# AFNO layers on one core: the MLP's products of a period put side by side, a second buffer for the spectrum's activation, and another order of the slots

## Chip, core and metric

One Trainium2 chip, and one of its cores. The metric is the device time of one execution of the whole program in microseconds (us), the median of several runs; lower is better.

## What is computed

The input is a batch of 4 images of 64 channels, 128 x 128, in fp32. One box-filter layer comes first, then four AFNO blocks, then two more box-filter layers. The change touches the AFNO blocks alone. One block, cut to what matters:

```python
xn = _ln(xp, ln1w, ln1b)                          # xp: channels last
xf = jnp.fft.rfft2(xn, axes=(1, 2), norm='ortho')
o1 = relu(complex product of xf with w1, + b1)    # 64 x 64 per frequency
o2 = complex product of o1 with w2, + b2
o2 = o2 * ((|o2r| > 0.01) | (|o2i| > 0.01))
x = residual + irfft2(o2)
xp2 = _ln(x, ln2w, ln2b)
h = jax.nn.gelu(xp2 @ mw1 + mb1, approximate=False)   # 64 -> 256
x = x + h @ mw2 + mb2                                 # 256 -> 64
```

Lines 3 to 5 are shortened to words: the reference writes the real and imaginary parts out.

## The kernel before

`afno_layers` holds all four blocks of all four images in one loop. A **run** n is one block of one image; there are 16 (`RUNS`). A run has 16 **periods** q (`BLOCKS`), and each period has four **slots** s. In period q of run n every engine carries one block of 8 image rows through one stage of the MLP of run n, and in its slots does parts of the Fourier work, mostly that of run n + 1 (`parts`, `parts_in`). So the MLP of one image and the spectrum of the next lie beside each other. Q = 16n + q numbers the MLP's blocks.

The MLP's pieces are, on TensorE (PE): `turn` (four 128-column transposes into `turned`, L1734), `mlp_up(Q, 0)` and `mlp_up(Q, 1)` (the two halves of the hidden layer, each two 512-column products on 64 rows of the array, into the one buffer `wide`, L1714), `mlp_down` (four 512-column products with 64 output rows, into `result`, L1725) and `turn_back` (transposes into `result`, L1740). ScalarE (ACT) does `gelu` out of `wide` (L1539), `operand` (the copy of `turned`, L1545), `mlp_delta` (the bias on `result`, L1552) and `square` (the squares for the layer norm's sums, L1573). VectorE (DVE) adds the result to the image in `residual` (L1428), sums the rows in `sum_up` (two reductions, L1445 and L1447) and takes the inverse root in `root` (12 small steps, L985 to L1005). GpSimd (POOL) does `normalise` (L1270), `next_y` (L1282) and `fold` (L1293, L1295).

`mlp_up(Q, 1)` writes `wide` and so waits for gelu(Q, 0), and `mlp_up(Q + 1, 0)` for gelu(Q, 1). `mlp_down(i)` waits for residual(i - 1), since both use `result`.

The Fourier work of a run goes over the slots of the period so:

- q 0, 1 (slot 3) and q 4 (slots 1 and 2): `inverse` 4 to 7 of run n. PE forms an even and an odd part of 8 rows (L1642, L1646). ACT copies the odd part to `odd` (L1495), DVE adds in three steps (L1366, L1367, L1371), and POOL subtracts `odd` from the upper rows (L1258), which frees `odd` for the next copy.
- q 4 (slot 3) to q 5 (slot 2): `forward`, 16 groups of four transforms (L1660), copied out to `g` by DVE and ACT in turn (L1126 to L1129 and L1502).
- q 5 (slot 3) to q 10 (slot 1): `spectrum`, steps t = 0 to 18. A step has on PE the second transform fh(t) (`dft_h`, L1689, into bank 0), the first mixing product mix1(t-1) (L1680, into bank 2) and the second mix2(t-2) (L1671, into bank 3). ACT does relu o1(t-1) (L1519) and then the copy xf(t) out of bank 0 (L1526). DVE adds a bias in o2(t-2) (L1397), and makes the mask of step t-3 (L1414, L1417); POOL applies it (L1308, L1312). mix1(t) waits for xf(t). fh(0) waits for all copies of `forward` and for a DVE memset (L1390) behind them.
- q 11: `backward`, 16 groups (L1704), copied out by DVE (L1422) and ACT (L1531).
- q 12 (slots 0, 1, 3) and q 13 (slot 1): `inverse` 0 to 3.

What sets the order is written out by hand: each engine has a loop over the periods that calls the MLP's pieces and `parts(n, q, s, ...)` in a fixed order, and every engine works its list in that order. PE's list, in a period of the spectrum, is mlp_up(Q, 0), slot 0, turn_back(Q-2), turn(Q+1), slot 1, mlp_up(Q, 1), slot 2, mlp_down(Q-1), slot 3. ACT's is gelu(Q, 0), slot 0, operand(Q+1), a square, slot 1, gelu(Q, 1), slot 2, mlp_delta(Q-1), slot 3. In runs whose layer is the last (`fresh`), ACT has copies of the next image besides (`fill_stage`, L1584).

## Time and profile before

| | |
|---|---|
| median of 3 runs | 3581.37 us (3580.07 to 3583.23) |
| the profiled execution's own time | 3576.51 us |
| its span | 3574.7 us |
| PE busy in the span | 3260.3 us (91%) |
| DVE, ACT, POOL busy | 2413.1, 2210.3, 1648.1 us (68%, 62%, 46%) |
| mean granted TensorE clock | 0.966 |

The profiled execution is 4.9 us below the median and 1.8 us above its own span. Busy times are sums over the whole program; matmuls are pipelined, so a busy PE may still be waiting inside a matmul's record. The AFNO part with its MLP lies from about 410 to 3160 us of the span.

### The profile page before, as it was taken

What the parts mean: (1) busy time and instruction counts of PE and PEld (TensorE: products, weight loads), DVE (VectorE), ACT (ScalarE), POOL (GpSimd) and SP (SyncE); (2) the same over time, 40 slices, a digit from 0 to 9 for tenths busy, and PEclk for the clock granted to TensorE, in tenths of its full rate; (3) what the DMA queues carried; (4) which work ended last, traced back from release to release, by engine and by line L of the source; (5) the groups of instructions that cost most, each with busy time, mean ns of one, the idle gap of its engine ahead of it and who ended that gap; (6) DMA issues with size and microseconds to landing.
All of it is one profiled execution on the core that took longest, in us unless ns stands there. A gap on an engine that the chain in (4) does not pass through costs nothing. (4 is left out here: it accounts for less than half of the span.)

```text
span 3574.7 us, 52777 instructions
## 1 busy us (share of the span) xinstructions
PE 3260.3 (91%) x18285; PEld 1965.9 (55%) x18285; DVE 2413.1 (68%) x4148; ACT 2210.3 (62%) x3477; POOL 1648.1 (46%) x1389
## 2 busy tenths in 40 slices
PE   6946699999999999998999999999999999979689
PEld 2735364647464646464646464646464646334257
DVE  4956676767676676666666767676767665636677
ACT  3954466666666666667666666666656565646468
POOL 4445545464645454545454545555454543210242
PEclk7968899999999999999999999999999999989889
DMA  9850001010101010313120101111111111356898
GB/s 326 273 183 24 30 31 65 31 65 31 65 30 65 30 65 30 118 48 142 48 89 31 65 30 65 36 65 41 55 42 54 42 54 42 138 193 188 265 301 239
DMA packets 250280, 334.08 MB, mean 93 GB/s; under 512 B 22305, under 2 KB 195617, under 8 KB 242609
## 3 DMA queue, kind: packets, MB, share of 16 engines
q1 hardware_dynamic: 241664, 315.29, 26.0%
...
## 5 line engine op out<-in xcount | busy, mean ns | idle before, releaser
L1539 ACT ACTIVATE images<-a_wide,a_up_b 128x1024 f32<-128x1024 f32 x512 | 569.4, 1112 | 187.9 <-PE a_wide L1714 186.5
L1714 PE MATMUL a_wide<-images 64*128 64x512 f32 x2048 | 579.7, 641 | 37.1 <-ACT images L1539 36.4
L1312 POOL TENSOR_TENSOR images<-a_o,a_mag 128x256 f32<-128x256 f32 (+1 forms) x512 | 360.8, 731 | 401.7 <-DVE a_mag L1417 401.7
L1725 PE MATMUL a_result<-images 128*64 128x512 f32 x2048 | 495.9, 604 | 31.9 <-DVE images L1428 31.7
L1270 POOL TENSOR_TENSOR images<-images,a_stat 128x512 f32<-128x512 f32 x256 | 268.2, 1049 | 520.4 <-DVEq L1462 503.3
L1397 DVE TENSOR_TENSOR a_o<-a_bank,a_mix_b 128x512 f32<-128x512 f32 (+1 forms) x272 | 181.1, 666 | 266.8 <-PE a_bank L1671 260.8
L1689 PEld LDWEIGHTS a_bank<-a_dft_h,a_g 128*128 128x128 f32 x2080 | 272.4, 191 | 129.0 <-issue 129.0
L1671 PEld LDWEIGHTS a_bank<-a_mix,a_o 128*128 128x128 f32 x2080 | 252.8, 191 | 149.7 <-issue 130.9
L1519 ACT ACTIVATE a_o<-a_bank,a_mix_b 128x512 f32<-128x512 f32 (+2 forms) x272 | 181.7, 668 | 202.9 <-PE a_bank L1680 202.9
L1671 PE MATMUL a_bank<-a_mix,a_o 128*128 128x128 f32 x2080 | 298.0, 285 | 5.4 <-DVE a_o L1397 3.2
L1725 PEld LDWEIGHTS a_result<-images 128*64 128x64 f32 x2048 | 128.0, 136 | 313.5 <-issue 290.5
L1447 DVE TENSOR_REDUCE a_stat<-a_sq 128x16 f32<-128x1024 f32 x240 | 290.3, 1210 | 9.4 <-ACT a_sq L1573 8.3
L1258 POOL TENSOR_TENSOR images<-images,a_odd 128x512 f32<-128x512 f32 (+1 forms) x128 | 161.6, 1262 | 288.4 <-DVE images L1367 279.4
L1660 PE MATMUL a_bank<-dft_w,images 128*128 128x128 f32 x2048 | 246.6, 279 | 48.1 <-POOL images L1295 46.1
L1552 ACT ACTIVATE images<-a_result,a_down_b 128x512 f32<-128x512 f32 x256 | 175.8, 687 | 185.4 <-PE a_result L1725 185.1
L1714 PEld LDWEIGHTS a_wide<-images 64*128 64x128 f32 x2048 | 157.3, 185 | 238.9 <-issue 202.6
L1445 DVE TENSOR_REDUCE a_stat<-images 128x16 f32<-128x1024 f32 x232 | 281.3, 1212 | 4.8
L1660 PEld LDWEIGHTS a_bank<-dft_w,images 128*128 128x128 f32 x2048 | 236.0, 193 | 83.7 <-POOL images L1295 46.1
L1428 DVE TENSOR_TENSOR images<-a_result,images 128x512 f32<-128x512 f32 x256 | 175.3, 685 | 156.0 <-PE a_result L1740 155.9
L1689 PE MATMUL a_bank<-a_dft_h,a_g 128*128 128x128 f32 x2080 | 277.3, 275 | 1.8 <-DVE a_g L1390 1.8
L1680 PE MATMUL a_bank<-a_xf,a_mix_fold 128*128 128x512 f32 (+1 forms) x544 | 270.0, 578 | 0.8 <-ACT a_xf L1526 0.8
L1573 ACT ACTIVATE a_sq<-images 128x1024 f32<-128x1024 f32 x216 | 227.5, 1053 | 66.5 <-DVE a_stat L1447 42.8
...
## 6 DMA issues: line engine op xcount, KB each, us to landing
...
```

The costliest lines, as they stand in the source:

```text
L1270: G.tensor_tensor(rows(y2[:, i % 2]), x[:, row:row + HB], r[:, :, None].broadcast_to([P, HB, C]), ALU.mult).then_inc(s_y2, 1)
L1312: ins = G.tensor_tensor(y[n % 2][:, :, to].rearrange("p c k -> p k c"), o2[:, j % 3, lo:4, r], mask[:, lo:4], ALU.mult)
L1445: V.tensor_reduce(stat[:, 0, r % SETS, kind - 1, u * SH:(u + 1) * SH], strip, AX.X, ALU.add)
L1447: V.tensor_reduce(stat[:, 1, r % SETS, kind - 1, u * SH:(u + 1) * SH], squares_of(r, kind, u), AX.X, ALU.add).then_inc(s_sq_read, 1)
L1539: A(hidden[:, i % 2, j], wide[:], ACT.Gelu, bias=up_b2[:, l, j:j + 1]).then_inc(s_hid, 1)
L1573: A(squares_of(r, kind, u), strip, ACT.Square).then_inc(s_sq, 1)
L1660: mm = M(bank[i % 4][:, c * P:(c + 1) * P], y[n % 2][:, 4 * i + c, :], dft_w[:], start=True, stop=True)
L1671: mm = M(bank[3][:, k * P:(k + 1) * P], o1[:, k * P:(k + 1) * P], mix2[:, l], start=True, stop=True)
L1680: M(bank[2][:, 0:cols], mix1_fold[:, l], xf[:, 0:cols], start=True, stop=True).then_inc(s_mix1, 1)
L1689: mm = M(bank[0][:, k * P:(k + 1) * P], g[:, first_kw(t) + k].rearrange("p r c -> p (r c)"), dft_h[:], start=True, stop=True)
L1714: mm = M(wide[:, half * BANK:(half + 1) * BANK], up_fold[cs, l, j * P:(j + 1) * P], yc[cs, i % 2], start=True, stop=True)
L1725: mm = M(result[half * C:(half + 1) * C, :], down[:, l, j, :], hidden[:, i % 2, j, half * BANK:(half + 1) * BANK], start=j == 0, stop=j == ...
```

## The change

1. **Order on PE.** mlp_up(Q, 1), mlp_down(Q-1) and mlp_up(Q+1, 0) are called one behind the other, after slot `window_after(q)` (3, but 2 in q 4 and 12, and 1 in q 5, where mlp_up(Q+1, 0) stays behind slot 3). ACT's gelu(Q, 1) and mlp_delta(Q-1) go to the same place.
2. **Order inside a spectrum step.** mix2(t-2) is called behind mix1(t-1) and fh(t), no longer ahead of them. `o1` has two homes (`o1_of`): the odd steps write it to `odd`. Relu o1(j) waits for mix2(j-2) instead of mix2(j-1).
3. **First slot.** Slot 0 is called ahead of the transposes (on DVE ahead of `residual`, on ACT ahead of `operand`) in q 5 to 10 and 12 (`SLOT_FIRST`), and behind them elsewhere. Of the slots 0 that hold work this moves that of q 11 on DVE and ACT alone.
4. **DVE's sums.** The two reductions of `sum_up` are called in two slots that follow each other, and the root of q 1 behind slot 2.

No instruction is added or taken out, apart from waits. In the diff below the pieces stand in this order: the tables, `o1_of`, DVE's loop, ACT's `inverse`, `spectrum` and loop, and PE's loop. PE's `spectrum` is left out: its block of mix2 (`j = t - 2`) moves as it is from the top to behind fh and reads `o1_of(j)`.

```diff
+SLOT_FIRST = (5, 6, 7, 8, 9, 10, 12)
+def window_after(q):
+    return {4: 2, 5: 1, 12: 2}.get(q, 3)
...
+        def o1_of(j):
+            return odd[:].rearrange("p h c -> p (h c)") if j % 2 else o1[:]
...
+                    late = 3 if q == 5 else 2 if q % 4 == 3 and fresh(n) else 1
...
+                        if s - late in (0, 1):
+                            for strip in strips[-1:]:
+                                sum_up(*strip, s - late)
...
-                            if q == 1 and s == 1:
+                            if q == 1 and s == 2:
                                 root(r, range(ROOT_STEPS))
...
                     act.wait_ge(s_x_up, INVERSES * n + j)
+                    if j == 0:
+                        act.wait_ge(s_mix2, N_CHUNK * (n + 1) - 1)
...
-                        if j >= 1:
-                            act.wait_ge(s_mix2, before + j)
+                        if before + j >= 2:
+                            act.wait_ge(s_mix2, before + j - 1)
+                        if j == 1 and n:
+                            act.wait_ge(s_x_up, INVERSES * n)
...
-                    parts(n, q, 1, inverse, forward, spectrum, backward)
-                    if mlp:
-                        gelu(Q, 1)
...
+                        if s == 1 and q == 12:
+                            for strip in strips_at(n, q)[:1]:
+                                square(*strip)
...
+                        if s == window_after(q):
+                            if 0 <= Q < BLOCKS * RUNS:
+                                gelu(Q, 1)
+                            if 0 <= Q - 1 < BLOCKS * RUNS:
+                                mlp_delta(Q - 1)
...
-                    parts(n, q, 1, inverse, forward, spectrum, backward)
-                    if mlp:
-                        mlp_up(Q, 1)
-                    parts(n, q, 2, inverse, forward, spectrum, backward)
-                    if 0 <= Q - 1 < BLOCKS * RUNS:
-                        mlp_down(Q - 1)
-                    parts(n, q, 3, inverse, forward, spectrum, backward)
+                    for s in range(4):
+                        if s or q not in SLOT_FIRST:
+                            parts(n, q, s, inverse, forward, spectrum, backward)
+                        if s == window_after(q):
+                            if 0 <= Q < BLOCKS * RUNS:
+                                mlp_up(Q, 1)
+                            if 0 <= Q - 1 < BLOCKS * RUNS:
+                                mlp_down(Q - 1)
+                        if s == max(window_after(q), 3 if q == 5 else 0) and 0 <= Q + 1 < BLOCKS * RUNS:
+                            mlp_up(Q + 1, 0)
```

What it does to the lists, at three places. The line numbers of the changed kernel differ: L1742 and L1753 are mlp_up and mlp_down, L1688 `forward`, L1708 fh, L1699 mix1, L1717 mix2, L1768 and L1762 turn_back and turn.

PE, from the last quarter of `forward` in q 5 to slot 1 of q 6; before:

```order
L1714 MATMUL a_wide<-images 128x512 x2
L1660 MATMUL a_bank<-dft_w,images 128x128 x16
L1725 MATMUL a_result<-images 64x512 x4
L1689 MATMUL a_bank<-a_dft_h,a_g 128x128
L1714 MATMUL a_wide<-images 128x512 x2
L1680 MATMUL a_bank<-a_xf,a_mix_fold 128x128
```

and now:

```order
L1742 MATMUL a_wide<-images 128x512 x2
L1753 MATMUL a_result<-images 64x512 x4
L1688 MATMUL a_bank<-dft_w,images 128x128 x16
L1708 MATMUL a_bank<-a_dft_h,a_g 128x128
L1742 MATMUL a_wide<-images 128x512 x2
L1699 MATMUL a_bank<-a_xf,a_mix_fold 128x128
```

mlp_down stood between the last group of `forward` and fh(0); now fh(0) is the next product behind that group.

PE, slots 1 to 3 of q 6 with the products of the MLP (the first row is turn); before:

```order
L1734 MATMUL a_turned<-ident,images 128x128 x4
L1671 MATMUL a_bank<-a_mix,a_o 128x128
L1680 MATMUL a_bank<-a_xf,a_mix_fold 128x512
L1689 MATMUL a_bank<-a_dft_h,a_g 128x128 x4
L1714 MATMUL a_wide<-images 128x512 x2
L1671 MATMUL a_bank<-a_mix,a_o 128x128 x4
L1680 MATMUL a_bank<-a_xf,a_mix_fold 128x512
L1689 MATMUL a_bank<-a_dft_h,a_g 128x128 x4
L1725 MATMUL a_result<-images 64x512 x4
```

and now:

```order
L1762 MATMUL a_turned<-ident,images 128x128 x4
L1699 MATMUL a_bank<-a_xf,a_mix_fold 128x512
L1708 MATMUL a_bank<-a_dft_h,a_g 128x128 x4
L1717 MATMUL a_bank<-a_mix,a_o 128x128
L1699 MATMUL a_bank<-a_xf,a_mix_fold 128x512
L1708 MATMUL a_bank<-a_dft_h,a_g 128x128 x4
L1717 MATMUL a_bank<-a_mix,a_odd 128x128 x4
L1699 MATMUL a_bank<-a_xf,a_mix_fold 128x512
L1708 MATMUL a_bank<-a_dft_h,a_g 128x128 x4
L1717 MATMUL a_bank<-a_mix,a_o 128x128 x4
L1742 MATMUL a_wide<-images 128x512 x2
L1753 MATMUL a_result<-images 64x512 x4
```

Three steps of the spectrum follow each other with no product of the MLP between; between fh(t) and mix1(t) stands mix2(t-2) alone.

ACT, from the first `inverse` of q 12 to slot 3; before:

```order
L1495 ACTIVATE a_odd<-a_bank 128x512 [waits a_x_up,a_iw]
L1545 ACTIVATE images<-a_turned 128x512 [waits a_up,a_tr]
L1495 ACTIVATE a_odd<-a_bank 128x512 [waits a_x_up,a_iw]
L1539 ACTIVATE images<-a_wide,a_up_b 128x1024 [waits a_up]
L1573 ACTIVATE a_sq<-images 128x1024 [waits a_sq_read,a_x]
L1552 ACTIVATE images<-a_result,a_down_b 128x512 [waits a_back,a_down]
```

and now:

```order
L1520 ACTIVATE a_odd<-a_bank 128x512 [waits a_mix2,a_x_up,a_iw]
L1572 ACTIVATE images<-a_turned 128x512 [waits a_up,a_tr]
L1520 ACTIVATE a_odd<-a_bank 128x512 [waits a_x_up,a_iw]
L1600 ACTIVATE a_sq<-images 128x1024 [waits a_sq_read,a_x]
L1566 ACTIVATE images<-a_wide,a_up_b 128x1024 [waits a_up]
L1579 ACTIVATE images<-a_result,a_down_b 128x512 [waits a_back,a_down]
```

The square, which waits for DVE's sums into x, now stands ahead of gelu(Q, 1). In q 4 both copies of the odd part stand ahead of gelu(Q, 1) in the same way; before, it stood between them.

## Rows read from the trace of the kernel before

**Rows 1.** Busy time by engine over one run; PE, PEld, DVE, ACT, POOL.

```profile
1121.00:1297.33 176.33, 170.98 (x972) 103.07 (x973) 123.39 (x216) 110.38 (x164) 91.06 (x77) 1.00 0.14 49
```

**Rows 2.** Timeline, PE, spectrum, q 7: start us, us, engine, line.

```profile
1194.35 1.05 PE L1689 MATMUL a_bank<-a_dft_h,a_g 128*128 128x128 f32 x8
1195.24 0.60 PE L1740 MATMUL a_result<-ident,images 128*128 128x128 f32 x4
...
1196.11 1.06 PE L1671 MATMUL a_bank<-a_mix,a_o 128*128 128x128 f32 x8
1197.00 1.02 PE L1680 MATMUL a_bank<-a_xf,a_mix_fold 128*128 128x512 f32 x2
1197.87 1.05 PE L1689 MATMUL a_bank<-a_dft_h,a_g 128*128 128x128 f32 x8
1198.85 1.13 PE L1714 MATMUL a_wide<-images 64*128 64x512 f32 x4
1199.91 1.16 PE L1671 MATMUL a_bank<-a_mix,a_o 128*128 128x128 f32 x8
```

**Rows 3.** Timeline, PE's turn and what ACT does behind it, q 6.

```profile
1180.32 0.60 PE L1734 MATMUL a_turned<-ident,images 128*128 128x128 f32 x4
...
1180.96 0.60 ACT L1545 ACTIVATE images<-a_turned 128x512 f32<-128x512 f32 x1 [0.27 <-PE a_turned L1734]
1181.45 1.05 ACT L1573 ACTIVATE a_sq<-images 128x1024 f32<-128x1024 f32 x1
...
1183.11 0.61 ACT L1526 ACTIVATE a_xf<-a_bank 128x512 f32<-128x512 f32 x1
```

**Rows 4.** Timeline, the first image's spectrum, which has no MLP beside it.

```profile
344.64 0.69 ACT L1519 ACTIVATE a_o<-a_bank,a_mix_b 128x512 f32<-128x512 f32 x1 [1.31 <-PE a_bank L1680]
345.38 1.16 PE L1671 MATMUL a_bank<-a_mix,a_o 128*128 128x128 f32 x8
```

**Rows 5.** Timeline, all engines, end of q 5.

```profile
1175.31 1.94 PE L1725 MATMUL a_result<-images 128*64 128x512 f32 x8
1175.42 1.33 ACT L1502 ACTIVATE a_g<-a_bank 64x252 f32<-64x252 f32 x4 [0.45 <-PE a_bank L1660]
...
1176.90 0.17 DVE L1390 MEMSET a_g<- 1x128 f32 x1 [0.82 <-ACT a_g L1502]
...
1177.22 0.46 PE L1689 MATMUL a_bank<-a_dft_h,a_g 128*128 128x128 f32 x2
```

**Rows 6.** Timeline, q 4.

```profile
1150.30 0.66 PE L1734 MATMUL a_turned<-ident,images 128*128 128x128 f32 x4 [1.09 <-POOL images L1270]
...
1157.19 0.60 ACT L1495 ACTIVATE a_odd<-a_bank 128x512 f32<-128x512 f32 x1 [2.29 <-POOL images L1258]
```

**Rows 7.** Timeline, q 12.

```profile
1274.30 1.94 PE L1725 MATMUL a_result<-images 128*64 128x512 f32 x8
1274.42 1.11 ACT L1539 ACTIVATE images<-a_wide,a_up_b 128x1024 f32<-128x1024 f32 x1
1274.67 0.69 DVE L1371 TENSOR_TENSOR images<-a_bank,images 128x512 f32<-128x512 f32 x1
...
1275.43 1.05 ACT L1573 ACTIVATE a_sq<-images 128x1024 f32<-128x1024 f32 x1
...
1276.17 1.13 PE L1642 MATMUL a_bank<-a_g,a_idft_e 128*128 128x512 f32 x2
```

**Rows 8.** Timeline: mlp_up and DVE's root in q 1, mlp_down in q 2.

```profile
1130.70 1.13 PE L1714 MATMUL a_wide<-images 64*128 64x512 f32 x4 [0.28 <-ACT images L1539]
...
1133.49 1.10 DVE L985 SCALAR_TENSOR_TENSOR a_stat<-a_stat 128x64 f32<-128x64 f32 x1
...
1140.26 1.94 PE L1725 MATMUL a_result<-images 128*64 128x512 f32 x8 [1.15 <-DVE images L1428]
```

**Rows 9.** Timeline, DVE, a mask of the spectrum beside POOL's work, and one without.

```profile
1195.02 0.29 DVE L1417 TENSOR_SCALAR a_mag<-a_mag 128x256 f32<-128x256 f32 x1
...
1198.53 1.94 DVE L1417 TENSOR_SCALAR a_mag<-a_mag 128x256 f32<-128x256 f32 x1
```

More of the change, by code:

```diff
@@ L1588, in _ @@
                     Q = BLOCKS * n + q
-                    mlp = 0 <= Q < BLOCKS * RUNS
-                    if mlp:
+                    if 0 <= Q < BLOCKS * RUNS:
                         gelu(Q, 0)
-                    parts(n, q, 0, inverse, forward, spectrum, backward)
+                    if q in SLOT_FIRST:
+                        parts(n, q, 0, inverse, forward, spectrum, backward)
                     if 0 <= Q + 1 < BLOCKS * RUNS:
                         operand(Q + 1)
-                    if q != 12 and not (q % 4 == 3 and fresh(n)):
-                        for strip in strips_at(n, q):
-                            square(*strip)
@@ L1664, in spectrum @@
                     before, l = N_CHUNK * n, layer_of(n)
-                    j = t - 2
-                    if 0 <= j < N_CHUNK:
-                        pe.wait_ge(s_o1, before + j + 1)
-                        if j >= 1:
-                            pe.wait_ge(s_o2, before + j)
-                        for k in range(chunk(j)):
-                            mm = M(bank[3][:, k * P:(k + 1) * P], o1[:, k * P:(k + 1) * P], mix2[:, l],
-                                   start=True, stop=True)
-                        mm.then_inc(s_mix2, 1)
                     j = t - 1
@@ L1691, in spectrum @@
                         mm.then_inc(s_fh, 1)
+                    j = t - 2
+                    if 0 <= j < N_CHUNK:
+                        pe.wait_ge(s_o1, before + j + 1)
+                        if j >= 1:
+                            pe.wait_ge(s_o2, before + j)
+                        for k in range(chunk(j)):
+                            mm = M(bank[3][:, k * P:(k + 1) * P], o1_of(j)[:, k * P:(k + 1) * P], mix2[:, l],
+                                   start=True, stop=True)
+                        mm.then_inc(s_mix2, 1)
                     if t == 8:
@@ L1753, in _ @@
                         turn(Q + 1)
[L1754 to L1762 removed]
+                    for s in range(4):
+                        if s or q not in SLOT_FIRST:
+                            parts(n, q, s, inverse, forward, spectrum, backward)
+                        if s == window_after(q):
+                            if 0 <= Q < BLOCKS * RUNS:
+                                mlp_up(Q, 1)
[3 more added lines that the diff above has]
+                            mlp_up(Q + 1, 0)
         clear(nc, sems)
```

73 lines of the change are left out of this document (36 added, 37 removed).

## The prediction

> **What bounds the kernel now.** I read the table of busy times first, then one run of the loop (16 periods), then its timeline instruction by instruction. In a run of 176.3 us PE is busy 171.0, and the clock is granted in full (1.00); the other engines are at 52 to 70% [rows 1]. So PE bounds the run, and what counts is (a) how densely its products follow each other and (b) where it waits. Run follows run in the timeline in nearly the same way, so every figure below is for one run and is multiplied by 15, the runs that have both an MLP and the next spectrum beside it (run 15 has no next one).
>
> PE's prices, start to start [rows 2]: mix1 0.87, fh 0.89, mix2 0.89, turn_back and turn 0.87 together, mlp_up 1.06. mlp_down takes 1.87, from its start to that of the next product [rows 7]. Before, the steps of the spectrum in q 6 to 9 are never next to each other: a product of the MLP or the transposes stands between each pair, and no product there shows an idle time [rows 2]. That cover is what the change takes away.
>
> **What is saved: changes of shape.** fh before mlp_up lasts 0.98 to the next start, but 0.89 before turn_back; mix2 lasts 1.16 behind mlp_up, but 1.06 behind turn [rows 2]. So going into the MLP's half-array products costs 0.09 and coming out 0.10, together 0.19 a stretch. By the loop there are 33 stretches a run before (16 of mlp_up(Q, 1), 7 of mlp_down apart from it, in q 4 to 9 and 11, and 10 of mlp_up(Q+1, 0) apart from mlp_down, in q 0, 1, 4 to 9, 11, 12) and 17 after (q 5 keeps two). 16 x 0.19 = **3.0 us saved**. The Trainium skill's TensorEngine Tiling (Array Packing), Key Properties, says that changing the tiling mode drains the array; mlp_up is tiled by rows and mlp_down by columns, so by that rule a merged stretch still drains between them, half of the saving goes, and the sum below rises by 1.5 a run. The rows here do not show such a drain: mlp_up takes 1.06 before mix2 [rows 2], and that is also what it takes before mlp_down elsewhere in the timeline.
>
> **What is saved in q 0 to 2.** `inverse` 4 and 5 now come ahead of mlp_up(Q, 1) and mlp_down, 1.06 + 1.87 = 2.9 us nearer to the transposes. That hides the wait for gelu(Q, 0) (0.28 in q 1 [rows 8]), and lets DVE do its additions earlier. At the end of this stretch mlp_down of q 2 waits 1.15 for DVE [rows 8], so the gain is DVE's: turn_back of q 1 comes 0.5 earlier, and from there the chain residual, two sums, root, `inverse` 5, residual is shorter by 0.3 because `inverse` 4 is no longer in it and by 0.85 if the root's first step (1.10 beside POOL's normalise [rows 8]) runs alone, in about a quarter of that as the steps behind it do. 1.6 in all, of which 0.4 was counted as shape: **1.2 saved**. Bounds 0.3 to 1.2.
>
> **What is lost, five waits.**
>
> *fh(0), q 5.* It needs the last copies of `forward` and the memset behind them. ACT's four copies of the last group begin 0.11 after mlp_down's start, the memset is at 1176.90, and fh(0) starts at 1177.22, 1.91 after mlp_down started, which itself took 1.87 of that [rows 5]. So mlp_down just covers the copies. Now nothing stands between the last group and fh(0): PE idles **1.9**. This one I take as certain.
>
> *mlp_up(Q+1, 0), q 4.* It needs gelu(Q, 1), and ACT now does both odd copies first. The second waits for POOL and starts 1157.19 - 1150.30 = 6.89 after turn [rows 6]; copy 0.60 [rows 6], gelu 1.11 [rows 7] and about 0.1 to PE put mlp_up at 8.6 to 8.7. PE would reach it at 0.44 + four 512-column products of 0.87 + 0.1 + 1.06 + 1.87 = 6.95. **1.7 lost**; behind it is `forward`, which moves with it. Bounds 1.0 (if POOL comes earlier) to 1.9.
>
> *mix1(2), q 6.* Behind turn ACT has operand, square, relu, xf. From turn's start operand comes at 0.64, the square at 1.13 and xf, with a relu before it and no gap, at 2.79; it ends at 3.40 [rows 3]. A result of ACT reaches PE's weight load 0.05 later (345.33 to 345.38 [rows 4]): 3.45. PE, with mix1(1), fh(2) and the one-column mix2(0) (a quarter of 0.89) is ready at 0.44 + 0.87 + 0.89 + 0.22 = 2.4. About 1.1 lost, and 0.15 for two smaller gaps as below: **1.2**. Before, mlp_up and a mix2 lay in there. Bounds 0.8 to 1.3.
>
> *q 7 to 9.* The same with a full mix2: PE wants the weights of mix1 at 0.44 + 0.87 + 0.89 + 0.89 less 0.11 for the load, 2.98 after turn; xf, behind operand, square and relu, is there at 3.3: 0.34. For steps that follow each other without a square: fh's record 1.05, latency 0.04, xf 0.60, latency 0.05 make 1.74 from fh's start, and the weights are wanted at 0.89 + 0.89 - 0.11 = 1.67: 0.07. So 0.41 a period, three times 1.2; all three shape savings of 0.38 are used up by it. For DVE in q 7: a mask that lasts 1.94 beside POOL's work, not 0.29 [rows 9], now lies in a slot of 2.7 us together with a bias add, a reduction and half of `sum_up` (1.2), which makes the next add, and mix2 two steps on, late by about 0.3. **1.5** together, bounds 0.6 to 4 (rival 3).
>
> *mlp_up(Q+1, 0), q 12.* gelu(Q, 1) now stands behind the square, and the square waits for DVE's third addition: it starts at 1275.43, whatever PE does [rows 7]. Square 1.0, gelu 1.11, 0.1 to PE: 1277.6. PE reaches the product at 1274.30 + 1.87 = 1276.17 [rows 7]. 1.45 lost. Then `inverse` 2 and 3 come later, ACT has a square and a gelu between their odd copies, so the second copy comes about 0.5 later still, DVE's sums wait for it and mlp_down of q 14 waits for DVE. With the shape saving of 0.2 given back there: **2.1**. Bounds 1.2 to 2.1: the waits of q 14 and 15 could take up some of it.
>
> The two homes of o1 cost nothing: `odd` is free long before. Splitting `sum_up` costs nothing; its halves lie under PE. Slot 0 of q 11 on DVE and ACT: their copies have 1.8 us for two groups of `backward`. In q 11 and 10 nothing is lost beyond 0.1.
>
> **Sum.** -3.0 - 1.2 + 1.9 + 1.7 + 1.2 + 1.5 + 2.1 = +4.2 us a run, 15 x 4.2 = 63. The profiled execution would go from 3576.5 to 3639.5, and the median, which lay 4.9 above it, from 3581.4 to **3644**. Left out are two runs where ACT has image copies of 2 us in the way (a few us more) and the first image's spectrum, whose steps get shorter by some 0.1 (under 2 us less). With all bounds at the low end the sum is +2.2 (-3.0 - 0.3 + 1.9 + 1.0 + 0.8 + 0.6 + 1.2), or with the q 0 to 2 gain in full +1.3; at the high end about +7.5.
>
> **Rivals.**
> 1. *The cover was never needed (faster).* If ACT's copies reach PE in time in q 4, 6 to 9 and 12, because PE drifts against ACT and each wait paid once moves the later ones into place, only fh(0) stays: -3.0 - 1.2 + 1.9 = -2.3, times 15 is -35: 3547. It is decided at mix1 behind a square: xf would have to end within 3.0 us of turn and not 3.4. For it: PE has 2.9 us more in one piece, in which ACT can catch up. Against it: operand, square, relu and xf come behind turn by order, back to back [rows 3]. 0.15.
> 2. *Only the waits outside the steps (about as before, or a little slower).* If the steps run at 2.64 with no gap and the rest holds, +4.2 - 2.7 = +1.5, or 3604: 0.16. If also q 4 costs nothing, -0.2, or 3578: 0.09.
> 3. *DVE becomes the bound.* The masks held by POOL cost 1.65 each more [rows 9]; in a slot with a sum DVE then has 4.5 us (add, reduction and mask 1.7, the hold 1.65, half a sum 1.2) against PE's 2.7, and mix2 two steps on is late by 0.9 instead of 0.3. Once in each of q 6 to 9 that is 2.7 a run more, 40 in all: 3684. For it: POOL works through q 6 and 7. Against it: the sum is now split, and the 4 us of the MLP let DVE catch up. 0.10.
>
> That the change does not do what it says I give no chance: the lists show it.
>
> **How the numbers follow.** My forecast has 0.50. Slower by over 0.2% (7 us, about what runs of this kernel can tell) is 0.50 + 0.16 + 0.10 = 0.76; within 0.2% is 0.09; faster is 0.15. The likeliest case alone gives 3612 (+2.1 a run) to 3670. The range takes in 3578, 3604 and 3684 and leaves out the faster case: 3575 to 3690.
>
> **What would show it.** In the new profile the run should last about 180.5 us, not 176.3. fh(0) should show 1.9 us idle behind a DVE memset; mlp_up in q 4 and 12 waits of 1.7 and 1.4 for ACT's gelu; mix1 small waits for xf, the largest, 1.1, in q 6; q 11 should be 0.4 shorter, and mlp_down of q 2 come 1.6 earlier. If mix1 shows no waits, rival 1 or 2 is right; if mix2 waits for DVE's add in q 6 to 9, rival 3.

## Result and the profile after

| | before | changed |
|---|---|---|
| median of 4 runs | 3581.19 us (3580.07 to 3583.23) | 3700.67 us (3693.03 to 3707.34) |
| ratio | | 1.0332, interval 1.0311 to 1.0353 |
| span of the profiled execution | 3574.7 us | 3705.6 us |
| PE, DVE, ACT, POOL busy | 3260.3, 2413.1, 2210.3, 1648.1 us | 3280.5, 2422.3, 2199.0, 1649.2 us |

It is 3.3% slower, in the direction forecast, but the loss is 119 us where 63 were forecast, and 3700.7 lies outside the range (3575 to 3690). PE's busy time rose by 20 us although its list does the same products with fewer changes of shape, and the runs of the changed kernel spread over 14 us, not 3. The first comes from the clock, as the experiments show; the second stays open. The profiled execution of the changed kernel (3707.3 us) is the slowest of its four, 6.7 us above the median, and what follows is read from it.

The waits of the changed kernel by PE in the loop of the layers (columns: engine, output and line that waited, what for; total us, times, longest us):

```profile
PE a_wide L1742 <- ACT images L1566: 79.0, 108, 3.1
PE a_result L1753 <- DVE images L1438: 40.4, 44, 2.0
PE a_bank L1699 <- ACT a_xf L1553: 39.9, 45, 1.2
PE a_turned L1762 <- POOL images L1280: 32.0, 27, 13.5
PE a_bank L1708 <- DVE a_g L1400: 29.3, 16, 1.8
PE a_bank L1732 <- POOL images L1322: 8.8, 16, 4.6
```

mlp_up's wait for gelu (L1742), mix1's for xf (L1699) and fh's for the memset (L1708) are new or larger, as forecast (36.4, 0.8 and 1.8 us before, in the same view). To see where a run loses its time I take the starts of `turn` from PE's timeline, one a period, and compare the distance from each to the next in both kernels (medians of eight runs without image copies; forecast from the terms of the prediction, each change of shape put in its period). A run takes 184.5 us, not 176.3.

| turn to turn | before | changed | difference | forecast |
|---|---|---|---|---|
| q 0 to 4 | 27.7 | 26.5 | -1.25 | -1.6 |
| q 4 to 5 | 16.09 | 17.39 | +1.31 | +1.3 |
| q 5 to 6 | 13.94 | 17.41 | **+3.47** | +1.7 |
| q 6 to 7 | 15.35 | 16.16 | +0.81 | +0.8 |
| q 7 to 8 | 16.47 | 17.35 | **+0.88** | +0.3 |
| q 8 to 9 | 16.02 | 16.01 | 0.0 | 0.0 |
| q 9 to 10 | 15.13 | 16.01 | **+0.88** | 0.0 |
| q 10 to 12 | 27.7 | 27.9 | **+0.18** | -0.4 |
| q 12 to 0 | 27.9 | 29.8 | +1.94 | +1.9 |
| run | 176.3 | 184.5 | +8.2 | +4.2 |

Four rows are as forecast, to 0.1 us; q 5, 7 and 9 hold 3.2 of the 4 us missed, and q 10 and 11 another 0.6. PE's timeline of the changed kernel in q 5, which answers to [rows 5], and the same stretch in windows (columns: window, its length, busy us and instructions of each engine, granted clock, DMA):

```profile
1209.78 3.62 PE L1688 MATMUL a_bank<-dft_w,images 128*128 128x128 f32 x31
1215.23 0.46 PE L1708 MATMUL a_bank<-a_dft_h,a_g 128*128 128x128 f32 x2 [1.83 <-DVE a_g L1400]
1215.62 1.78 PE L1742 MATMUL a_wide<-images 64*128 64x512 f32 x4
1217.34 0.79 PE L1699 MATMUL a_bank<-a_xf,a_mix_fold 128*128 128x128 f32 x2
1217.92 1.75 PE L1708 MATMUL a_bank<-a_dft_h,a_g 128*128 128x128 f32 x8
1219.51 0.60 PE L1768 MATMUL a_result<-ident,images 128*128 128x128 f32 x4
```

```profile
1213.00:1215.20 2.20, 0.40 (x4) 0.21 (x2) 1.31 (x5) 1.30 (x4) 0.00 (x0) 1.00 0.00 0
1215.20:1217.00 1.80, 1.77 (x6) 0.60 (x6) 1.80 (x2) 0.28 (x1) 0.00 (x0) 0.71 0.03 9
1217.00:1219.00 2.00, 2.00 (x10) 1.67 (x9) 1.72 (x7) 1.37 (x2) 0.00 (x0) 0.50 0.00 0
1219.00:1219.60 0.60, 0.60 (x5) 0.60 (x5) 0.00 (x0) 0.00 (x0) 0.00 (x0) 0.69 0.00 0
1219.60:1223.00 3.40, 3.00 (x21) 2.28 (x19) 1.05 (x3) 3.01 (x6) 0.00 (x0) 1.00 0.00 0
```

The idle before fh(0) is 1.83 us, as forecast. But right behind it the granted clock goes from 1.00 (2.4 GHz) to 0.50 (1.2 GHz), and mlp_up takes 1.78 us, not 1.13, and fh(1) 1.75, not 1.05. Before, the clock was 1.00 from 432 to 3180 us. In the changed kernel it falls in q 5 in 13 of 15 runs, and five times more in runs 6 to 8, in or behind PE's waits of 2.0 to 3.1 us around the image copies.

ACT in q 7, which answers to [rows 3], DVE's residual there, and what PE's mix1 does:

```profile
1236.74 0.60 ACT L1572 ACTIVATE images<-a_turned 128x512 f32<-128x512 f32 x1 [1.17 <-PE a_turned L1762]
1238.13 1.06 ACT L1600 ACTIVATE a_sq<-images 128x1024 f32<-128x1024 f32 x1 [0.79 <-DVE images L1438]
```

```profile
1235.87 0.69 DVE L1407 TENSOR_TENSOR a_o<-a_bank,a_mix_b 128x512 f32<-128x512 f32 x1 [2.82 <-PE a_bank L1717]
...
1237.20 0.29 DVE L1427 TENSOR_SCALAR a_mag<-a_mag 128x256 f32<-128x256 f32 x1
1237.41 0.68 DVE L1438 TENSOR_TENSOR images<-a_result,images 128x512 f32<-128x512 f32 x1
```

```profile
1240.30 1.12 PE L1699 MATMUL a_bank<-a_xf,a_mix_fold 128*128 128x512 f32 x2 [0.95 <-ACT a_xf L1553]
```

In q 7 and 9 the square reads the image that `residual` writes. DVE does slot 0's add, reduction and mask first, and the add waits for mix2, which now comes last in slot 0. So the square waits 0.79, xf comes as much later, and mix1 waits 0.95, not the 0.34 forecast for any square. In q 8, where the square does not wait for `residual`, the period is as long as before.

q 4 and 12, where the forecast held (ACT's second odd copy and PE's mlp_up in q 4; PE in q 12):

```profile
1192.04 0.60 ACT L1520 ACTIVATE a_odd<-a_bank 128x512 f32<-128x512 f32 x1 [3.89 <-POOL images L1268]
```

```profile
1193.79 1.13 PE L1742 MATMUL a_wide<-images 64*128 64x512 f32 x4 [1.63 <-ACT images L1566]
...
1319.96 1.13 PE L1742 MATMUL a_wide<-images 64*128 64x512 f32 x4 [1.36 <-ACT images L1566]
```

Two smaller waits, the first product of `backward` in q 11 and mlp_down in q 14:

```profile
1292.51 14.56 PE L1732 MATMUL a_bank<-a_dft_hi,images 128*128 128x128 f32 x128 [0.28 <-POOL images L1322]
...
1333.55 1.94 PE L1753 MATMUL a_result<-images 128*64 128x512 f32 x8 [1.33 <-DVE images L1438]
```

The first, for POOL's mask, is not there in an ordinary run before; the second was 0.88. So of the 1.94 lost in q 12 to 15 some 0.45 lies in q 14, where the prediction had it too.

### The profile page after: what moved, and what is told of

Same layout as the page of the kernel before. It is cut to its first block and busy times, and to the rows that moved or that the text cites. A ratio compares the mean times of both kernels' runs of the same rounds, so it can differ in the third digit from the quotient of the medians.

```text
span 3705.6 us, 52776 instructions
## 1 busy us (share of the span) xinstructions
PE 3280.5 (89%) x18285; PEld 1989.3 (54%) x18285; DVE 2422.3 (65%) x4148; ACT 2199.0 (59%) x3477; POOL 1649.2 (45%) x1389
## 5 line engine op out<-in xcount | busy, mean ns | idle before, releaser
L1742 PE MATMUL a_wide<-images 64*128 64x512 f32 x2048 | 586.3, 648 | 81.5 <-ACT images L1566 79.0
L1753 PE MATMUL a_result<-images 128*64 128x512 f32 x2048 | 498.5, 607 | 40.4 <-DVE images L1438 40.4
L1708 PEld LDWEIGHTS a_bank<-a_dft_h,a_g 128*128 128x128 f32 x2080 | 284.0, 199 | 147.3 <-issue 147.3
L1742 PEld LDWEIGHTS a_wide<-images 64*128 64x128 f32 x2048 | 158.8, 186 | 369.0 <-issue 352.7
L1753 PEld LDWEIGHTS a_result<-images 128*64 128x64 f32 x2048 | 128.4, 136 | 380.0 <-issue 380.0
L1699 PE MATMUL a_bank<-a_xf,a_mix_fold 128*128 128x512 f32 (+1 forms) x544 | 292.6, 621 | 40.8 <-ACT a_xf L1553 39.9
L1708 PE MATMUL a_bank<-a_dft_h,a_g 128*128 128x128 f32 x2080 | 288.4, 283 | 29.3 <-DVE a_g L1400 29.3
L1688 PE MATMUL a_bank<-dft_w,images 128*128 128x128 f32 x2048 | 241.6, 278 | 47.3 <-POOL images L1305 46.2
L1688 PEld LDWEIGHTS a_bank<-dft_w,images 128*128 128x128 f32 x2048 | 233.9, 193 | 71.5 <-POOL images L1305 46.3
L1732 PE MATMUL a_bank<-a_dft_hi,images 128*128 128x128 f32 x2048 | 235.3, 277 | 8.8 <-POOL images L1322 8.8
L1732 PEld LDWEIGHTS a_bank<-a_dft_hi,images 128*128 128x128 f32 x2048 | 232.2, 194 | 12.7 <-POOL images L1322 12.7
L1376 DVE TENSOR_TENSOR images<-a_bank,images 128x512 f32<-128x512 f32 x128 | 88.1, 688 | 202.1 <-PE a_bank L1674 147.4
```

Source lines behind the costliest of these rows:

```text
L1688: mm = M(bank[i % 4][:, c * P:(c + 1) * P], y[n % 2][:, 4 * i + c, :], dft_w[:], start=True, stop=True)
L1699: M(bank[2][:, 0:cols], mix1_fold[:, l], xf[:, 0:cols], start=True, stop=True).then_inc(s_mix1, 1)
L1708: mm = M(bank[0][:, k * P:(k + 1) * P], g[:, first_kw(t) + k].rearrange("p r c -> p (r c)"), dft_h[:], start=True, stop=True)
L1732: mm = M(bank[i % 4][:, c * P:(c + 1) * P], y[n % 2][:, 4 * i + c, :], dft_hi[:], start=True, stop=True)
L1742: mm = M(wide[:, half * BANK:(half + 1) * BANK], up_fold[cs, l, j * P:(j + 1) * P], yc[cs, i % 2], start=True, stop=True)
L1753: mm = M(result[half * C:(half + 1) * C, :], down[:, l, j, :], hidden[:, i % 2, j, half * BANK:(half + 1) * BANK], start=j == 0, stop=j == ...
```

## Experiments

Three questions: does the idle in q 5 bring the lower clock; does each wait belong to one edit; and what is left of the change if each is repaired. Where an expectation says step 5, it means period q 5. The table gives for each kernel the difference to the kernel before, us per run, by the same turns, and in how many of the 15 periods q 5 of its profiled execution the clock fell. Each batch of runs had the kernel before beside it, at 3577.7 (a), 3580.2 (b), 3579.7 (c), 3579.4 (d) and 3579.2 us (e), and at 3581.2 beside the changed kernel; so a difference of medians between batches is sure to some 4 us only.

| kernel | median | q 0-4 | q 4 | q 5 | q 6 | q 7 | q 8 | q 9 | q 10-11 | q 12-15 | low clock in q 5 |
|---|---|---|---|---|---|---|---|---|---|---|---|
| changed | 3700.7 | -1.3 | +1.3 | +3.5 | +0.8 | +0.9 | 0 | +0.9 | +0.2 | +1.9 | 13 of 15 |
| a1 MLP ahead of fh(0) | 3650.5 | -1.3 | +1.3 | -0.2 | +0.8 | +0.9 | 0 | +0.9 | +0.2 | +1.9 | 0 |
| a2 idle alone | 3614.6 | 0 | 0 | +1.9 | 0 | 0 | 0 | 0 | 0 | 0 | 5 |
| a3 gelu first, q 12 | 3666.1 | -1.2 | +1.3 | +1.9 | +0.8 | +0.9 | 0 | +0.9 | +0.2 | +0.5 | 5 |
| a4 stretch between, q 4 | 3709.4 | -1.3 | +1.5 | +3.5 | +0.8 | +0.9 | 0 | +0.9 | +0.2 | +1.9 | 12 |
| b1 residual first | 3745.7 | -1.3 | +1.3 | +5.7 | +0.8 | 0 | 0 | 0 | +1.2 | +2.6 | 10 |
| b2 square later | 3661.0 | -1.3 | +1.3 | +1.9 | +0.5 | +0.6 | -0.3 | -0.3 | +0.2 | +1.9 | 3 |
| b3 all five | 3664.4 | -1.2 | +1.5 | +2.0 | +0.5 | -0.3 | -0.3 | -0.3 | +1.2 | +0.8 | 8 |
| c1 residual in 7, 9 | 3665.8 | -1.3 | +1.3 | +1.9 | +0.8 | 0 | 0 | 0 | +0.2 | +1.9 | 2 |
| c2 repaired | 3597.5 | -1.3 | +1.3 | -0.2 | +0.5 | -0.3 | -0.3 | -0.3 | +0.2 | +0.5 | 0 |
| c3 repaired, apart in 4, 12, 13 | 3567.7 | -1.3 | 0 | -0.2 | +0.5 | -0.3 | -0.3 | -0.3 | +0.2 | 0 | 0 |
| b4 merged in 0, 1, 11 only | 3558.6 | -1.3 | 0 | 0 | 0 | 0 | 0 | 0 | -0.4 | 0 | 0 |
| c4 new order, not merged | 3607.9 | 0 | 0 | 0 | +0.1 | 0 | 0 | 0 | +1.8 | 0 | 0 |
| d1 best | 3551.0 | -1.3 | 0 | -0.2 | 0 | -0.3 | -0.3 | -0.3 | +0.2 | 0 | 0 |

(q 5 is the median of the runs: 15.80 us where the clock stayed at 1.00, 17.1 to 17.4 where it fell, 13.94 before. b1 has 18.00 without a fall and b3 15.94; both have another idle stretch in q 5, told below.)

**The idle and the clock: a1 and a2.** a1 changes one number of the changed kernel:

```diff
-    return {4: 2, 5: 1, 12: 2}.get(q, 3)
+    return {4: 2, 5: 2, 12: 2}.get(q, 3)
```

> The changed kernel, with mlp_up and mlp_down of step 5 ahead of the first forward stretch, so that TensorE works while VectorE's memset runs. Theory: TensorE's 1.83 us idle in front of fh(0) costs its own 1.9 us a run, and the fall of the granted clock to 0.50 that follows it costs another 1.6 us. Both go: 3.5 us in each of 15 runs, 52 us, about 3648 us, and no stretch below clock 1.00 behind step 5. Rival: the clock falls for another reason (the load of the run's start); then the idle goes and the fall stays: 28 us, about 3672 us. Second rival: mlp_down ahead of the forward stretches only waits for gelu in place of the memset; then under 10 us.

Measured 3650.5 us (3649.6 to 3651.6), 50 less than the changed kernel (47 if each is taken against the kernel before in its own batch), and PE's busy time is 3250.7 us, 30 less. PE has no idle there and the clock is 1.00:

```profile
1193.26 1.13 PE L1742 MATMUL a_wide<-images 64*128 64x512 f32 x4
...
1196.18 0.49 PE L1708 MATMUL a_bank<-a_dft_h,a_g 128*128 128x128 f32 x2
1196.60 1.13 PE L1742 MATMUL a_wide<-images 64*128 64x512 f32 x4
```

```profile
1196.20:1199.60 3.40, 3.40 (x25) 2.52 (x24) 2.53 (x9) 2.67 (x5) 0.00 (x0) 1.00 0.02 5
```

a2 makes the same idle in the kernel before, whose other waits are few (on PE, and the same for ACT's mlp_delta):

```diff
+                    if q == 5 and 0 <= Q - 1 < BLOCKS * RUNS:
+                        mlp_down(Q - 1)
                     parts(n, q, 2, inverse, forward, spectrum, backward)
-                    if 0 <= Q - 1 < BLOCKS * RUNS:
+                    if q != 5 and 0 <= Q - 1 < BLOCKS * RUNS:
                         mlp_down(Q - 1)
```

> The kernel before, with only step 5 changed: its mlp_down goes out ahead of slot 2, in one stretch, so that nothing stands between the last product of slot 1 and fh(0). Theory (idle and clock): 1.9 plus 1.6 us in each of 15 runs, 52 us slower than before, about 3633 us, and a stretch at clock 0.50 in each run where there was none. Rival (the clock falls only with the changed kernel's other load): 28 us slower, about 3609 us, clock 1.00 throughout. Second rival (the idle is absorbed later in the step): no change, 3581 us.

Measured 3614.6 us: 37 slower than before, between the two. Two neighbouring runs of its timeline, and windows: behind fh(0) of the first, then ahead of the fall and behind it in the second:

```profile
1188.75 0.46 PE L1691 MATMUL a_bank<-a_dft_h,a_g 128*128 128x128 f32 x2 [1.83 <-DVE a_g L1390]
1189.14 1.13 PE L1716 MATMUL a_wide<-images 64*128 64x512 f32 x4
...
1366.91 0.46 PE L1691 MATMUL a_bank<-a_dft_h,a_g 128*128 128x128 f32 x2 [1.83 <-DVE a_g L1390]
1367.30 1.34 PE L1716 MATMUL a_wide<-images 64*128 64x512 f32 x4
1368.57 0.80 PE L1682 MATMUL a_bank<-a_xf,a_mix_fold 128*128 128x128 f32 x2
```

```profile
1189.50:1193.00 3.50, 3.50 (x26) 2.56 (x23) 3.29 (x10) 2.43 (x6) 0.00 (x0) 1.00 0.02 5
1363.20:1367.70 4.50, 2.67 (x21) 2.28 (x22) 3.35 (x9) 2.88 (x9) 0.00 (x0) 1.00 0.00 0
1367.70:1371.20 3.50, 3.50 (x16) 2.63 (x13) 2.70 (x8) 1.47 (x3) 0.00 (x0) 0.56 0.02 5
```

The same idle of 1.83 us is followed by a fall in one run and not in the next; in 5 of 15 runs in all. An idle run costs 1.86 us without a fall (net of the one change of shape that a2 saves) and about 1.5 more with one: 15 x 1.86 + 5 x 1.5 = 35, of 37 measured. So filling the idle takes the falls in q 5 away (a1: 13 to none), the idle alone brings falls into a kernel that had none there (a2), but it is not enough.

It is not fh(0) that matters either. b3 has a1's edit and so no idle ahead of fh(0), but PE waits 1.94 us for copies of `forward` earlier in q 5, and the clock falls in 8 of its 15 periods behind that wait. Two neighbouring runs, with a fall and without, and their windows:

```profile
1191.12 9.04 PE L1687 MATMUL a_bank<-dft_w,images 128*128 128x128 f32 x64 [1.93 <-DVE a_g L1139]
...
1372.96 7.41 PE L1687 MATMUL a_bank<-dft_w,images 128*128 128x128 f32 x64 [1.94 <-DVE a_g L1139]
```

```profile
1191.20:1195.20 4.00, 4.00 (x22) 4.00 (x23) 2.94 (x8) 0.84 (x3) 0.00 (x0) 0.58 0.12 42
1373.10:1377.10 4.00, 4.00 (x37) 4.00 (x38) 3.83 (x11) 1.56 (x5) 0.00 (x0) 1.00 0.10 33
```

The waits of 1.63 in q 4 and 1.36 in q 12 are followed by no fall in any ordinary run of the changed kernel.

In a3, b2 and c1 nothing ahead of fh(0) in q 5 is different, the idle is there, and there are 5, 3 and 2 falls instead of 13: an edit elsewhere in the run that changes its length changes how many. Within one execution they are not scattered: in the changed kernel only runs 6 and 7, those with image copies, have none, and in a2 they come in runs 2, 5, 7, 10 and 13. What decides it, I leave open. The spread of the changed kernel's runs is not explained by it: a1, without falls in q 5, spreads over 2 us, but so do a2 with 5 (1.7 us) and a4 with 12 (1.2 us), while a3 and b2, with 5 and 3, spread over 6 and 8.

**One wait, one edit: a3, a4, b1, b2.** a3 puts gelu(Q, 1) of q 12 ahead of the square.

```diff
                         if s == 1 and q == 12:
+                            if 0 <= Q < BLOCKS * RUNS:
+                                gelu(Q, 1)
                             for strip in strips_at(n, q)[:1]:
                                 square(*strip)
```

> The changed kernel, with the gelu of step 12 ahead of the spectrum's square on ScalarE. Theory: steps 12 to 15 lost 1.9 us a run because TensorE's merged MLP stretch waits for that gelu; 28 us come back, about 3672 us. Rival: the square is then late for VectorE's root and the inverse products, and the loss moves there: within 7 us of the changed kernel, about 3700 us. A third of each would be 3690 us.

Measured 3666.1. q 12 to 15 lost 1.94 and now loses 0.5: 1.43 x 15 = 21 us, and the other 13 come from q 5, by fewer falls. So the theory held for three quarters of its term; the last 0.5 is not gelu's: mlp_down of q 14 still waits 1.33.

a4 moves the MLP's stretch of q 4, with its gelu, between the two odd copies (`4: 1` in the table of `window_after`).

> The changed kernel, with the gelu of step 4 between the two odd copies on ScalarE, not behind both. Theory: TensorE's wait of 1.6 us in step 4 goes in 15 runs: 25 us, about 3676 us. Rival: the second odd copy comes later by the gelu's time and the odd products wait for it: within 7 us of the changed kernel, about 3700 us.

Measured 3709.4, no gain. The wait for gelu is gone, but PE does `inverse` 7 behind the stretch, ACT's second odd copy comes 8.3 behind `turn`, not 6.9, and `forward` waits for DVE instead, 0.32 and 1.03 us:

```profile
1194.84 2.05 PE L1688 MATMUL a_bank<-dft_w,images 128*128 128x128 f32 x16 [0.32 <-DVE images L1381]
1197.92 3.84 PE L1688 MATMUL a_bank<-dft_w,images 128*128 128x128 f32 x32 [1.03 <-DVE a_g L1139]
```

b1 puts DVE's `residual` ahead of slot 0 in every period:

```diff
-                    if q in SLOT_FIRST:
-                        parts(n, q, 0, inverse, forward, spectrum, backward)
                     if 0 <= Q - 2 < BLOCKS * RUNS:
                         residual(Q - 2)
-                    if q not in SLOT_FIRST:
-                        parts(n, q, 0, inverse, forward, spectrum, backward)
+                    parts(n, q, 0, inverse, forward, spectrum, backward)
```

> The changed kernel, with VectorE's residual ahead of slot 0's add, reduce and mask. Theory: in steps 7 and 9 ScalarE's square waits 0.79 us for the residual, which stands behind an add that waits for mix2, and mix1 waits 0.6 us longer than in step 8 for it: 1.2 us in each of 15 runs, 18 us, about 3683 us. Rival: slot 0's mask then comes later and its release of the buffers with it, mix1 waits all the same for ScalarE's own queue: within 7 us, about 3700 us.

Measured 3745.7, 45 slower. The gain is there, 0.89 in q 7 and in q 9, and more than lost in q 5, 10 and 12, which I had not costed. In q 5 the copies of `forward` stand behind a residual that waits for `turn_back`, and PE waits for the copies:

```profile
1210.70 5.46 PE L1685 MATMUL a_bank<-dft_w,images 128*128 128x128 f32 x32 [1.94 <-DVE a_g L1139]
```

With two idle stretches in q 5, inside `forward` and ahead of fh(0), the clock falls in 10 of its 15 periods, and twice in four of them.

c1 does the edit in q 7 and 9 alone.

> The changed kernel, with VectorE's residual ahead of slot 0 in steps 7 and 9 alone; steps 5, 6, 8, 10 and 12 keep slot 0 first. Theory: the edit that made all steps slower together had won 0.89 us in step 7 and 0.89 in step 9 and lost 2.2 in step 5, 1.0 in step 10 and 0.7 in step 12, where copies or masks that TensorE waits for stood behind the residual. Placed in 7 and 9 alone it wins 1.8 us in each of 15 runs: 27 us, about 3674 us. Rival: the gain of 7 and 9 was paid for in step 10 (the masks come later), which stays: 3689 us or more.

Measured 3665.8, 35 less than the changed kernel: q 7 and 9 are back at the kernel before, 1.78 x 15 = 27, and there are 11 fewer falls, worth 16; between the two profiled executions lie 41. That the order of `residual` and slot 0 makes the whole loss of q 7 and 9 is shown.

b2 puts ACT's squares of q 6 to 9 behind slot 1 (`if s == (1 if 6 <= q <= 9 else 0) and ...`).

> The changed kernel, with the squares of steps 6 to 9 behind slot 1's relu on ScalarE. Theory: the new waits of mix1 for that relu (1.0 us in step 6, 0.95 in 7 and 9, 0.34 in 8) come from the square ahead of it; they go: 3.2 us in each of 15 runs, 48 us, about 3652 us. Rival (VectorE is the bound there): the root that needs the square is late in its place and the step keeps its length: within 10 us, about 3695 us.

Measured 3661.0, 40 less. 2.0 us a run come from q 6 to 9, 30 in all, not 3.2 a run; the rest is the fewer falls. The waits of mix1 fall from 39.9 us to 11.7, and some reappear as waits of mix2 for DVE's add, 12.7 where 4.8 were:

```profile
PE a_bank L1717 <- DVE a_o L1407: 12.7, 15, 2.9
PE a_bank L1699 <- ACT a_xf L1553: 11.7, 21, 1.2
```

**Together: b3 and c2.** b3 is a1, a3, a4, b1 and b2 in one.

> The changed kernel with all five single edits at once: MLP stretch of step 5 ahead of fh(0), gelu ahead of the square in step 12, gelu between the odd copies in step 4, residual ahead of slot 0, squares of 6 to 9 behind slot 1. Theory (each new wait has a cause of its own): 3.5 + 1.9 + 1.7 + 3.2 = 10.3 us a run less than the changed kernel, 154 us, about 3547 us, below the kernel before. Rival (the waits cover one another, or VectorE becomes the bound): half of it, about 3620 us.

Measured 3664.4: far above the theory's 3547, and above the rival's 3620 too, since a4 and b1 (as it stood) each cost, and b1's wait in q 5 brings the falls back that a1 takes away. c2 is a1, a3, b2, c1, and slot 0 of q 11 ahead on DVE and ACT as before.

> The changed kernel with a repair of each wait, each in its own step: the MLP stretch of step 5 ahead of fh(0), gelu ahead of the square in step 12, residual ahead of slot 0 in 7 and 9 on VectorE, squares behind slot 1 in 6 to 9, slot 0 ahead in step 11 on VectorE and ScalarE as it was before. By the turn-to-turn times of the single edits: steps 0 to 2 -1.3, 4 +1.3, 5 -0.2, 6 +0.5, 7 to 9 -0.8, 10 and 11 -0.2, 12 to 15 +0.5 against the kernel before, -0.2 us a run in all, about 3577 us. Rival (the repairs work only with the slack that the other waits leave, and new ones appear): a third of the changed kernel's loss stays, about 3620 us.

Measured 3597.5: 18 above the kernel before in its batch, so 102 of the 119 us are back. The turn-to-turn times are as added up except in q 10 and 11, which did not gain; and the two runs with image copies take 22 us more than two others, where they took 9 before.

**What pays: b4, c3, c4.** b4 is the kernel before with slots 2 and 3 called ahead of the MLP's products and gelu in q 0, 1 and 11 only.

> The kernel before, with the MLP products in one stretch in steps 0, 1 and 11 alone, where gelu is early. Theory: the merged stretch pays where its operand is ready: 1.3 us in steps 0 to 2 and 0.4 in 11, 1.7 us in each of 15 runs, 26 us faster than before, about 3555 us. Rival: what steps 0 to 2 won came from slot 0's new place, not from the merged stretch; then within 5 us of the kernel before, 3581 us.

Measured 3558.6 (3554.8 to 3560.5), ratio 0.994 [0.9926, 0.9953]: faster than before, in just the places expected, -1.3 and -0.39 a run. The rival, that q 0 to 2 had won by slot 0's place, is out. The merged stretch does save, where its operand is early.

c3 is c2 with the products apart as before in q 4, 12 and 13.

> The repaired kernel with the MLP products apart again in steps 4, 12 and 13, as before the change. Theory: what is left of the loss lies there (1.3 us in step 4, 0.5 in 12 to 15): 1.8 us a run less, about 3550 us, some 30 us below the kernel before and at or below the kernel that merges in steps 0, 1 and 11 alone (3558.6 us). Rival: steps 13 to 15 lose their 0.6 us to something else (the split sums of VectorE): about 3560 us.

Measured 3567.7, ratio 0.9966 [0.9952, 0.998]. q 4 and 12 to 15 are back at the kernel before, so their whole loss was the merging. A normal run takes 174.7 us, as in b4; the rest is in the runs with image copies.

c4 is the change without its merging: everything of the diff but `window_after`, with slot 0 ahead throughout on DVE and ACT as before.

> The kernel before with everything of the change but the merging: mix2 behind fh, two homes for the activation, sums split over two slots, the root of step 1 a slot later; the MLP products stand apart and slot 0 ahead as before. Theory: under the cover of the MLP products the new order costs nothing in steps 4 to 9, within 0.5 us a run, 3574 to 3590 us; the whole loss comes from taking the cover away. Rival: mix2 last in its slot delays VectorE's add and mask by itself (the residual and the square of steps 7 and 9, the last masks of step 10): 0.9 + 0.9 + 0.5 us a run, 35 us, about 3616 us.

Measured 3607.9, between the two. The steps of q 4 to 9 cost 0.1, as the theory had it, but 1.76 a run are lost in q 10 and 11. PE's and DVE's timeline in q 10:

```profile
1254.49 1.13 PE L1722 MATMUL a_bank<-a_mix,a_o 128*128 128x128 f32 x8 [1.19 <-DVE a_o L1410]
```

```profile
1253.21 0.23 DVE L1014 SCALAR_TENSOR_TENSOR a_stat<-a_stat 128x64 f32<-128x64 f32 x1
1253.65 0.69 DVE L1410 TENSOR_TENSOR a_o<-a_bank,a_mix_b 128x512 f32<-128x512 f32 x1 [0.21 <-DVE a_stat L1014]
```

mix2(16) waits for an add that stands behind the end of the root. Three runs ask why: d2 and e1 put mix2 first again from step t = 17 and from 16, e3 puts DVE's two sums together again.

> The kernel with the step order alone, and mix2 first again in the steps t = 17 and 18 only. That kernel lost 1.26 us in step 10 and 0.50 in step 11, where mix2(16) waited 1.19 us for VectorE's add, which stood behind the end of the root. Theory: that add is late because mix2(15) comes last in its step; both losses go, 1.76 us in each of 15 or 16 runs: about 3580 us, within 0.2% of the kernel before. Rival: the add waits for the root whenever the mix comes (sums and root lie later because the sums are split): the loss stays, about 3608 us; half of each would be 3594 us.

> The kernel with the step order alone, and mix2 first again from t = 16. The run with mix2 first from t = 17 still lost 1.8 us in steps 10 and 11: mix2(16) waits for an add that stands behind the second half of the root, which stands behind the add of mix2(14), the product of t = 16. Theory (order): with mix2(14) 2 us earlier that add, the root's half and the next add come earlier: 1.8 us in 15 runs go, about 3580 us. Rival (sums): the root's halves are late because one of VectorE's two sums, 1.2 us, now stands in the slot of the first half; the loss stays, 3608 us, and the run with the sums together shows it instead.

> The kernel with the step order alone, and the two sums together in one slot again. Theory (order): the root's second half still waits behind the late add of mix2(14), the loss of 1.8 us a run in steps 10 and 11 stays, 3608 us. Rival (sums): the first half of the root comes 1.2 us earlier, and the loss goes: about 3580 us.

Measured 3607.7, 3599.9 and 3610.7. Neither t = 17 nor the sums change anything; from t = 16 the loss falls by 0.4 to 1.36. So the order has a part in it, and the split sums have none. That it works through DVE's chain of adds and root halves, and that this chain begins earlier than I moved it, is a reading of the timeline and not shown; 1.36 us stay open.

**The runs with image copies: d3.** In the changed kernel gelu(Q, 1) of q 3 and 15 stands behind a copy (1.99) and a square, and mlp_up waits:

```profile
1550.52 1.99 ACT L1611 ACTIVATE a_stage<-images 128x1024 f32<-128x1024 f32 x1 [1.55 <-POOL images L1292]
1552.54 1.06 ACT L1600 ACTIVATE a_sq<-a_stage 128x1024 f32<-128x1024 f32 x1
1553.50 1.10 ACT L1566 ACTIVATE images<-a_wide,a_up_b 128x1024 f32<-128x1024 f32 x1
```

```profile
1554.74 2.08 PE L1742 MATMUL a_wide<-images 64*128 64x512 f32 x4 [3.14 <-ACT images L1566]
```

It also takes 2.08 then, not 1.13: the clock is low behind this idle too.

> The changed kernel, with the gelu of periods 3 and 15 ahead of the image copy and the square on ScalarE in the two fresh runs. Theory: there mlp_up(Q+1, 0) waits 3.1 us for a gelu that stands behind a copy of 1.99 us and a square of 1.06; four such waits of 2.5 to 3.1 us go: 10 to 12 us, about 3690 us. Rival: the copy is then late for the sums and the root, whose readers wait instead: 3695 to 3701 us, no difference that can be told.

Measured 3695.3 (3693.2 to 3696.7). In the trace q 3 of that run goes from 9.93 to 7.47 and the three runs around it lose 5.9 us less; but the two medians' ratios, 1.0322 [1.0306, 1.0338] and 1.0332 [1.0311, 1.0353], cannot be told apart.

**Best version: d1 and e2.** d1 is c3 with q 6 apart too and its square back in place, mix2 first for t up to 4 and from 17, and d3's edit. e2 has mix2 first from 16.

> The repaired kernel with MLP products apart in steps 4, 6, 12 and 13, mix2 first again in the steps t up to 4 and from 17, and the gelu of periods 3 and 15 ahead of the image copy in the two fresh runs. Theory (costs and gains have fixed places and add up): steps 0 to 2 -1.3, 5 -0.2, 6 0, 7 to 9 -0.8, 10 and 11 -0.4 against the kernel before: 2.7 us a run, 40 us, about 3541 us, below the 3558.6 us of the kernel that merges in 0, 1 and 11 alone. Rival: steps 10 and 11 keep 0.2 us and step 6 0.5 us, 2.0 us too slow by the sum: about 3555 us.

> The best kernel so far (3551 us) with mix2 first from t = 16 in place of 17. It lost 0.5 to 0.6 us a run in steps 10 and 11 against the kernel that merges in 0, 1 and 11 alone. Theory (order): that goes, 8 us, about 3543 us. Rival (sums, or the residual of step 11): it stays, within 3 us of 3551 us.

d1: 3551.0 us (3548.3 to 3553.2), ratio 0.992 [0.9907, 0.9934], the fastest seen: 28 us below the kernel before in its batch and 150 below the changed one, nearer the rival's 3555 than the theory's 3541. A normal run takes 174.1 us, not the 173.6 expected: q 10 and 11 did not gain. e2: 3557.7, worse. q 10 and 11 gained as expected (-0.4, from +0.2), but mix2(14), now next to mix2(13), waits 1.00 for DVE, in q 9, and 1.2 a run are lost there. So the order does reach q 10 and 11, but part of the gain may be a wait paid one period earlier:

```profile
1225.22 1.06 PE L1705 MATMUL a_bank<-a_mix,a_odd 128*128 128x128 f32 x8
1227.28 1.13 PE L1705 MATMUL a_bank<-a_mix,a_o 128*128 128x128 f32 x8 [1.00 <-DVE a_o L1410]
```

## Why the prediction was right and wrong

The direction, the five waits and the path through PE were right, and of q 4, 6 and 12 the sizes too. What failed are three terms of the sum. fh(0) in q 5 was priced as 1.9 us of idle with the clock at 1.00 behind it; with the shape it saves the period should have lost 1.7, and it lost 3.5. The 1.5 for q 7 to 9, shape aside, measured 2.9, because the square waits for DVE's `residual`, a wait that the ACT chain did not have. And "in q 11 and 10 nothing is lost beyond 0.1" was wrong by 0.6.

- **fh(0), q 5, 1.9 "taken as certain":** the idle is 1.83, and with the saved change of shape the period costs 1.86 (a2), 1.7 forecast. The term failed by what followed it: a second cost of about 1.5 us, the clock, in 13 of 15 runs. The prediction read the clock as 1.00 and priced every product at it, also behind an idle stretch that its rows did not contain. Some 20 of the missing 56 us.
- **q 7 to 9, 1.5 a run:** right in q 8 (0.0), wrong in q 7 and 9. The prediction took the ACT chain of q 6 [rows 3] for all three and put 0.3 on DVE's mask. It did not ask what the square reads: in q 7 and 9 it reads what `residual` has just written, and `residual` stands behind an add whose mix2 the change makes later. 1.43 a run, 21 us; c1 takes it back. The 0.3 for the mask beside POOL is not seen: in c1 q 7 is as long as before, like q 8.
- **q 10 and 11, -0.4:** +0.18. The saving is real (b4: -0.39), and 0.57 is lost beside it. c4 shows that what the change has beside the merging costs here, and only here (1.76), and e2 that with mix2 first from t = 16 these periods do gain 0.4; the 0.28 that `backward` waits for POOL's mask is gone there too. The rest was not followed.
- **q 0 to 3:** -1.25, not -1.6. mlp_down of q 2 still waits, 0.96 us where it was 1.15 [rows 8]. b4 gives the same -1.3 with nothing but the merging. The 0.3 missing is the root's first step, which was to take about a quarter of 1.10 once it runs apart from POOL's normalise; it takes 0.57 (0.58 in b4), so 0.53 is saved there, not 0.85:

```profile
1168.87 0.57 DVE L991 SCALAR_TENSOR_TENSOR a_stat<-a_stat 128x64 f32<-128x64 f32 x1
```

- **q 4, 6 and 12:** +1.31, +0.81, +1.94 against 1.3, 0.8, 1.9. The waits of q 4 and 12 are 1.63 and 1.36, forecast 1.7 and 1.4; that of q 6 shows as 0.79, forecast 1.1, and the period came out all the same, so there the agreement is in the sum and not in the wait. c3 shows that q 4 and 12 are the merging alone.
- **Changes of shape, -3.0:** not seen by itself. It is inside each interval that came out right, and in q 11 alone it shows bare, 0.39 for two stretches saved: 0.19 each, as in the sum. The Trainium skill's rule that the prediction named (TensorEngine Tiling (Array Packing), Key Properties), by which the merged stretch still drains between its two tilings, would have given half of that; the trace does not bear out a cost there.
- **Runs with image copies, "a few us more":** the runs 6 to 8 together lost 6 us beyond what ordinary runs lose. The clock is low five times there, in q 2, 3 and 15, where before it never fell.
- **Rivals:** the first two fell, since the waits came. The third, DVE as the bound at the mask beside POOL's work, is not what held q 7 and 9, though b2 shows DVE next in line in q 7 (mix2 waits for its add there). The range missed because its upper end was set by rival 3's 3684, where the high end of the prediction's own bounds, +7.5 a run, is 3694 already; and nothing in either stood for the clock, or for a wait that the list of five did not have.
